# Moving one half of one of eight states between engines in a recurrent-scan and mixture-of-experts kernel

## The reference

```python
def step(state, inp):
    x_t, dt_t, B_t, C_t = inp
    dA = jnp.exp(dt_t[:, :, None] * A[None])
    state = state * dA + (dt_t * x_t)[:, :, None] * B_t[:, None, :]
    y_t = jnp.einsum('bds,bs->bd', state, C_t)
    return (state, y_t)
```

## Time and profile before

| what | us |
|---|---|
| median of 3 runs | 1773.71 |
| lowest, highest | 1764.98, 1775.46 |
| the profiled execution, its time | 1772.78 |
| the profiled execution, its span | 1771.0 |
| DVE busy | 1616.0 (91%) |
| PE busy | 1560.3 (88%) |
| POOL busy | 1440.2 (81%) |
| ACT busy | 1405.2 (79%) |

### The profile page before, as it was taken

One profiled execution on the slowest core, in us unless ns is written; L12 is line 12 of the kernel. 1 busy time (PEld: TensorE's weight loads), 2 busy tenths in 40 slices (PEclk: granted clock), 3 DMA queues, 4 the chain that ended last, 5 costly groups with the idle time before them and its releaser, 6 DMA issues. The chain is left out here.

```text
span 1771.0 us, 43319 instructions
## 1 busy us (share of the span) xinstructions
PE 1560.3 (88%) x13334; PEld 806.2 (46%) x13334; DVE 1616.0 (91%) x1808; ACT 1405.2 (79%) x2640; POOL 1440.2 (81%) x716
## 2 busy tenths in 40 slices
PE   5775589999999999999999999989998989999888
PEld 5422344444444444444544444444444444444444
DVE  5787689999999999999999999999998999999987
ACT  4797587887887788887888788788888788888882
POOL 1365578898988888988898888888998899989976
PEclk9898699999999999999999999999999999999999
DMA  8667656575666775576566566565466454764633
GB/s 240 208 225 220 167 121 139 137 168 167 139 138 139 183 154 134 136 181 158 138 141 162 172 142 135 139 146 145 91 135 157 131 127 97 154 141 107 141 80 79
DMA packets 209432, 261.82 MB, mean 148 GB/s; under 512 B 26826, under 2 KB 105428, under 8 KB 209172
## 3 DMA queue, kind: packets, MB, share of 16 engines
q1 hardware_dynamic: 205236, 252.04, 58.9%
q0 software_dynamic: 4096, 8.40, 1.6%
HBM read 216.32 MB, written 43.79 MB: 147 GB/s over the span
## 5 line engine op out<-in xcount | busy, mean ns | idle before, releaser
L702 POOL TENSOR_TENSOR arena<-arena 128x1024 f32<-128x1024 f32 x512 | 1201.5, 2360 | 201.7 <-DVE arena L1210 160.0
L1210 DVE TENSOR_TENSOR_SCAN arena<-arena,ps 128x512 f32<-128x512 f32 x944 | 1085.7, 1203 | 56.4 <-POOL arena L702 27.2
L961 ACT ACTIVATE arena<-arena,neg_A 128x512 f32<-128x512 f32 (+1 forms) x944 | 630.5, 713 | 88.6 <-DVE arena L1210 84.9
L1418 PE MATMUL ps<-arena 128*64 128x128 f32 x6912 | 471.7, 281 | 118.3 <-DVE arena L1210 92.8
L1432 PE MATMUL ps<-arena,ident 64*64 64x512 f32 x4096 | 559.4, 618 | 1.7 <-POOL arena L702 1.6
L1418 PEld LDWEIGHTS ps<-arena 128*64 128x64 f32 x6912 | 376.1, 138 | 351.8 <-DVE arena L1210 177.6
L1192 DVE TENSOR_TENSOR ps<-arena,ps 128x512 f32<-128x512 f32 x512 | 325.2, 681 | 12.1 <-PE ps L1404 12.0
L967 ACT ACTIVATE arena<-ident,b_turned 128x128 f32<-128x128 f32 x864 | 273.1, 387 | 0.0
L1432 PEld LDWEIGHTS ps<-arena,ident 64*64 64x64 f32 x4096 | 108.0, 132 | 181.9 <-issue 175.1
L902 ACT ACTIVATE arena<-ps,arena 128x256 f32<-128x256 f32 x160 | 67.2, 471 | 112.3 <-PE ps L1502 112.2
L674 POOL DMA_INDIRECT x_rms_by_expert<-arena,slots x64 | 69.4, 1085 | 89.0 <-DMA x_rms_by_expert<-arena,slots 50.0
(11 more groups left out here) (168 smaller groups left out, 1018.6 us busy)
## 6 DMA issues: line engine op xcount, KB each, us to landing
arena<-c_scratch SPq DMA_DIRECT2D x128, 1024.0 KB, 8.6
arena<-w_routed_scaled SPq DMA_DIRECT2D x40, 256.0 KB, 2.8
arena<-in_L_ffn_W_r_dram SPq DMA_DIRECT2D x40, 256.0 KB, 8.9
arena<-c_scratch SPq DMA_DIRECT2D x40, 256.0 KB, 3.5
arena<-w_shared_tiles SPq DMA_DIRECT2D x128, 64.0 KB, 7.8
x_rms_by_expert<-arena SPq DMA_DIRECT2D x1, 5120.0 KB, 27.8
arena<-x_rms_by_expert SPq DMA_DIRECT2D x40, 128.0 KB, 2.6
routed_by_expert<-arena SPq DMA_DIRECT2D x40, 128.0 KB, 8.5
```

The lines of the kernel that those rows point to most:

```text
L702: nc.gpsimd.tensor_tensor(products[:, i % RING, :, :], states[:, i % 2, :, :], c_rows[:, i // CG, i % CG, :].unsqueeze(1).broadcast_to((P, ...
L961: nc.scalar.activation(decay[:, 2 * i + h, :], dflat[:, ds(slot + h * L, L)], ACT.Exp, scale=aflat[:, ds(col, 1)]).then_inc(s["decay_ready ...
L1210: vector.tensor_tensor_scan(states[:, i % 2, h, :], decay[:, m, :], ps[bank][:], 0.0, ALU.mult, ALU.add).then_inc(s["scanned"], 1)
L1418: ins = mm(bank[HP * r:HP * r + HP, c * P:(c + 1) * P], u_turned[:, odd, c, h * P + HP * r:h * P + HP * r + HP], diag[:, c, :], start=True ...
```

## The change

State 5 of a group with blocks gets a new kind Q. Its first half stays as in D: TensorE broadcasts B, VectorE multiplies by u, in place. For its second half GpSimd makes u*B in SBUF (`u_q`, 128x512) after product 3, from a second row of `b_row`, and ScalarE writes the decay to PSUM (`q_decay_to_psum`) after scan (4,0). VectorE thus makes seven products a group with blocks instead of eight. The B rows are laid out by state instead of by group, `c_scratch` gets eight more rows, and a group with a block loads two rows into `b_row` in two DMAs of 256 KB. The load waits for the second product too. `evict_block` moves from step 4 to step 5 of ScalarE's loop. `b_rest` in the first stage moves to other memory, its first write waits for `c_copied` instead of `b_first_made`, and the store of C is two DMAs. The plan of banks for groups with blocks changes by itself: before it was (0,2,1) (1,0,2) (1,2,0) (1,0,2) (2,1,0) (2,0,1) (1,2,0) (0,1,2) and it becomes (2,0,1) (1,2,0) (1,0,2) (1,2,0) (0,1,2) (2,0,1) (1,2,0) (0,1,2).

```diff
-    KIND = ("DEDDEDEE", "DEDDEDEP")
+    KIND = ("DEDDEDEE", "DEDDEQEP")
...
-    DECAYS = (SCANS, SCANS - NH)
+    DECAYS = (SCANS, SCANS - NH - 1)
...
-        b_row = take(L)
+        b_row = take(2 * L, "p (n t) -> p n t", n=2)
+        u_q = take(L)
...
             def store_c(b):
                 sp.wait_ge(s["c_copied"], b + 1)
-                sp.dma_start(c_d[:, b * L:(b + 1) * L], c_new[0:C_B_ROWS, :]).then_inc(s["c_stored"], 16)
+                sp.dma_start(c_d[0:C_B_ROWS, b * L:(b + 1) * L], c_new[0:C_B_ROWS, :]).then_inc(s["c_stored"], 16)
+                sp.dma_start(c_d[C_B_ROWS:, b * L:(b + 1) * L], c_new[Q_ROW:Q_ROW + E, :]).then_inc(s["c_stored"], 16)
...
             def load_b_row(u, g, tb):
                 if not isinstance(u, int) or u:
                     sp.wait_ge(s["u_b_pooled"], u)
-                sp.dma_start(b_row, c_d[S:C_B_ROWS][ds(g, 1), ds(tb, L)].broadcast_to((P, L))).then_inc(s["b_row_loaded"], 16)
+                    sp.wait_ge(s["u_q_pooled"], u)
+                for n in range(2):
+                    sp.dma_start(b_row[:, n, :], c_d[S + n * E:S + (n + 1) * E][ds(g, 1), ds(tb, L)].broadcast_to((P, L))
+                                 ).then_inc(s["b_row_loaded"], 16)
...
-                        pool.wait_ge(s["b_row_loaded"], (b * E + g) * 16 + 16)
+                        pool.wait_ge(s["b_row_loaded"], (b * E + g) * 32 + 32)
...
+                    if blocks and i == Q_AT - 2:
+
+                        nc.gpsimd.tensor_tensor(u_q, u_in.rearrange("p n h t -> p (n h t)")[:, ds(slot_q, L)], b_row[:, 1, :],
+                                                ALU.mult).then_inc(s["u_q_pooled"], 1)
...
-                nc.scalar.copy(c_new, ps[6][0:B_ROW, :]).then_inc(s["c_copied"], 1)
+                nc.scalar.copy(c_new, ps[6][:]).then_inc(s["c_copied"], 1)
...
+            def q_decay_to_psum(u, g, slot):
+
+                act.sem_inc(s["q_bank_claimed"], 1)
+                col = snap(g * SG + (S + Q_AT))
+                nc.scalar.activation(ps[BANKS[True][Q_AT][1]][:], dflat[:, ds(slot + L, L)], ACT.Exp,
+                                     scale=aflat[:, ds(col, 1)]).then_inc(s["q_decay_ready"], 1)
...
-                    if i == 4 and block_before:
+                    if i == Q_AT and block_before:
                         evict_block(u - 1)
...
-                        if KIND[block][i] == "P":
+                        if block_before and (i, h) == (Q_AT - 1, 0):
+                            q_decay_to_psum(*before)
+                        if KIND[block][i] == "P" or (KIND[block][i] == "Q" and h):
                             continue
...
             def first_rest(b):
-                dve.wait_ge(s["b_first_made"], b + 1)
+                dve.wait_ge(s["c_copied"], b + 1)
...
-                        for bank in (held, new):
+                        for bank in (held, new) if KIND[block][i] == "D" else (new,):
                             h = 0 if bank == first else 1
                             vector.tensor_tensor(ps[bank][:], uflat[:, ds(slot + h * L, L)], ps[new][:],
                                                  ALU.mult).then_inc(s["u_b_multiplied"], 1)
...
+                        if KIND[block][i] == "Q" and h:
+                            dve.wait_ge(s["u_q_pooled"], u + 1)
+                            dve.wait_ge(s["q_decay_ready"], u + 1)
+                            vector.tensor_tensor_scan(states[:, i % 2, h, :], ps[bank][:], u_q, 0.0, ALU.mult, ALU.add
+                                                      ).then_inc(s["scanned"], 1)
+                            continue
```

More of the change, by code:

```diff
@@ L58, in mamba_gated_moe @@
     N_SUM = SG
-    KIND = ("DEDDEDEE", "DEDDEDEP")
-    P_AT = SG - 1
-    assert KIND[1].index("P") == P_AT and "P" not in KIND[0]
+    KIND = ("DEDDEDEE", "DEDDEQEP")
+    P_AT, Q_AT = SG - 1, KIND[1].index("Q")
+    assert KIND[1].index("P") == P_AT and not set("PQ") & set(KIND[0])
     D_AT = [[i for i in range(SG) if kind[i] == "D"] for kind in KIND]
@@ L69, in mamba_gated_moe @@
     ND, NE = [len(at) for at in D_AT], [len(at) for at in E_AT]
-    ROW_OF = [i for i in range(SG) if "D" in (KIND[0][i], KIND[1][i])]
+    ROW_OF = [i for i in range(SG) if set("DQ") & {KIND[0][i], KIND[1][i]}]
     COL_OF = E_AT[1] + [i for i in E_AT[0] if i not in E_AT[1]]
@@ L650, in _ @@
             by_g = lambda a: a.rearrange("p h (g i) -> p h g i", g=E)
-            runs = []
             for k, i in enumerate(ROW_OF):
[L653 to L658, removed]
+                nc.gpsimd.tensor_copy(cb_sb[:, :, B_ROW + k * E:B_ROW + (k + 1) * E].unsqueeze(3), by_g(bp_sb[:])[:, :, :, i:i + 1]
                                       ).then_inc(s["bp_parted"], 1)
@@ L664, in _ @@
                                   ).then_inc(s["bp_parted"], 1)
[L665 removed]
+            assert NROW + NE[1] + 1 == N_PARTED
             pool.wait_ge(s["slots_made"], 1)
@@ L693, in gate_attn, with group @@
                 nc.gpsimd.tensor_tensor(s_times_g, gate_silu, attn_in, ALU.mult).then_inc(s["product_s_g_ready"], 1)
-            def group(b, g, blocks, slot=None):
+            def group(b, g, blocks, slot=None, slot_q=None):
                 n = b * S + g * SG
@@ L1184, in group @@
                         dve.wait_ge(s["dt_u_loaded"], b * 32 + 32)
-                    if KIND[block][i] == "D":
-                        k = D_AT[block].index(i)
+                    if KIND[block][i] in "DQ":
+                        k = sum(kind in "DQ" for kind in KIND[block][0:i + 1])
                         new = second if first == held else first
-                        dve.wait_ge(s["b_broadcast"], states_to(u, ND, block, k + 1))
+                        assert KIND[block][i] == "D" or (first, second) == (new, held)
+                        dve.wait_ge(s["b_broadcast"], states_to(u, BROADCASTS, block, k))
                         dve.wait_ge(s["scanned"], m0 + (2 * i + SCANS - 1))
-                        for bank in (held, new):
+                        for bank in (held, new) if KIND[block][i] == "D" else (new,):
                             h = 0 if bank == first else 1
@@ L1202, in group @@
                             continue
[L1203 to L1206, removed]
+                        if KIND[block][i] == "Q" and h:
[4 more added lines that the diff above has]
+                            continue
+                        dve.wait_ge(s["decay_ready"],
+                                    states_to(u, DECAYS, block, m + (0 if block and i > Q_AT else 1)))
+                        if KIND[block][i] in "DQ":
+                            done = PRODUCTS_TO[block][i] - (1 if KIND[block][i] == "D" and bank == held else 0)
+                            dve.wait_ge(s["u_b_multiplied"], states_to(u, PRODUCTS, block, done))
                         else:
@@ L1536, in group @@
                         ahead_g, ahead_t0, ahead_odd = next_g, next_t0, next_odd
-                    if ahead and KIND[ahead[3]][ahead[1]] == "D":
-                        bcast(*ahead, snap(ahead_g * NROW + ROW_OF.index(ahead[1])), ahead_t0)
+                    if ahead and KIND[ahead[3]][ahead[1]] in "DQ":
+                        bcast(*ahead, snap(ahead_g + ROW_OF.index(ahead[1]) * E), ahead_t0)
                     elif ahead and KIND[ahead[3]][ahead[1]] == "E":
```

31 lines of the change are left out of this document (19 added, 12 removed).

## The result

The changed kernel takes 1898.84 us (median of 4, 1890.97 to 1902.44) where the kernel before takes 1774.59 us (4 runs): 1.0708 times as long, 95% interval 1.0676 to 1.0739. The prediction was 1837, with a range of 1812 to 1885. The direction and the place are right, the size is half of what came: 124 us where 63 were summed.

The account below looks back on a forecast made before the run. VectorE is busiest, GpSimd paces half a group, and late half 0 of C closes a loop: 1.7 us in 35 groups (60) plus 3 for four gives 1772.8 + 63 = 1836, median 1837, range 1812 to 1885.

Parts of the forecast that it names:

- what bounds: Groups with blocks: GpSimd sets the pace in the second half; half 0 of C has 3.4 us to spare, loses 4.8.
- VectorE's saved product: VectorE, state 5: saves 0.59 us a group, but by the engines alone only 0.03 is left, 1 us in all.
- hidden: Rival: half 0 of C lands in time for product 0, so no change, 1772 us; chance 12%.
- the loop: GpSimd's product 0 through `u_q`, then the load of C back to product 0: period 25.5 us instead of 23.77.
- The four groups that follow the first group of a sequence: Groups with more slack before product 0: 0.2 us there, no more than 1.7 in any; 3 us taken for the four.
- The new wait for `c_copied`: First stage: met before a wait VectorE already has; with the extra stores nothing to 1 us, taken as 0.
- the landing of half 0 of C: DMA from issue to landing: 8.4 us from one load, plus 0.3 for bytes and burst still in flight.
- the first group: Start of the groups with blocks: no added time in the sum, which counts loads for groups 1 to 39.
- from E to the issue of C: SyncE's queue: E is the end of `u_q`, after product 3; half 0 of C goes out 3.80 us later.
- the burst: Loads undrained ahead of C, with the second row's 256 KB: nothing to 1.5 us, 0.3 taken.
- much slower: Rival: W2 and x also hold up TensorE, or C lands 10.1 us or more after issue: 1913 us; chance 10%.
- The stall by x: ScalarE's `copy_x_block` ahead of the second P decay: late x delays the scan 0.7 us, hidden behind the wait for product 0.

Follow-up runs that it names:

- the row behind C: Changed kernel with the second row of `b_row`, and its wait for `u_q`, loaded behind half 0 of C: 1770.68 us, 1.0007 times the kernel before.
- the wait alone: Kernel before, with the load of `b_row` also waiting for product 3 of the group before, no extra bytes: 1786.1 us, 1.0105 times the kernel before.
- the bytes alone: Kernel before, with a second 256 KB load behind each load of `b_row` and the old wait: 1769.65 us, 1.0003 times the kernel before.
- C ahead of x: Changed kernel, with half 0 of C loaded right behind the `b_row` rows, ahead of x, W1 and its bias: 2127.68 us, 1.2017 times the kernel before.

## Why the prediction was right, and where it was wrong

**Right: what bounds.** That GpSimd sets the pace in half a group, that VectorE's saved product is nearly worthless by itself, and that half 0 of C had less slack than it would lose, all stood. (It had 3.4 us in that group, 3.15 in the median, of which 0.3 pass anyway from landing to product 0; it goes out 5.2 us later, not 4.8.) The version with the row behind C is the rival "hidden" made real: 1771 against its 1772. That they agree so well is luck: 6.6 us gained in the groups pay for some 5 lost in the first, and the rival had neither.

**Right: the loop.** From product 0 to the end of u_q: 12.89 us summed, 12.87 in the group shown. u_q: 1.25 summed, a step of 1.24 (738.75 to 739.99, where product 4 starts). The four groups that follow the first group of a sequence lost 1.8 us together, where 3 was taken from the earlier trace rows. The new wait for `c_copied` and the extra stores cost nothing: the first products of the groups begin at 186.08 us after, 186.20 before.

**What failed** is sizes in the sum, not the mechanism: above all the landing of half 0 of C, put at 8.7 us where it took 9.4, with two smaller terms beside it, and the first group, put at nothing where it cost 6.

**Wrong: from E to the issue of C.** 3.80 summed from the steps in the earlier trace rows, 4.20 measured. Two terms: the step from the bias to C, which the earlier trace rows can't show since C waited there for product 3; I took 0.58 from the step between two other loads, and it is 0.80 (743.42 to 744.22). And E to x, 2.04 summed, is 2.21.

**Wrong, and the largest: the landing.** I took 8.4 and 0.3 for what is still in flight. The median from issue to landing of half 0 is 9.4 us over 39 groups (8.1 to 10.3), where it was 8.7 before (7.2 to 9.6), and 10.0 in the group shown. 8.4 was one load, on the short side. What I gave 0.3 costs 0.7, and the runs say which part of it does: where the same loads go out closer together but without the second row (the wait alone), the landing is 8.8; where the second row goes out behind C and all ahead of C is as before (the row behind C), it is 9.3. So it is the second row's 256 KB, ahead of C or just behind it, and not the tighter burst. x tells the same: 3.8 us after and 2.6 before, in the median, 2.6 with the wait alone and 4.1 with the bytes alone. From landing to product 0 another 0.3 passes, for which I had 0.1.

The sum closes over the 34 groups counted above (means): product 0 to the end of product 3 11.90, u_q 1.24, to the issue of C 4.25, landing 9.38, to product 0 0.32, together 27.09. Summed were 11.64, 1.25, 3.80, 8.7 and 0.1: 25.49. So of 1.6 us that were missing the landing is 0.7, the issue 0.4, the step to product 0 0.2. The last 0.3 is for the most part in five groups, in which GpSimd stands once more between product 0 and product 3, by 1.2 to 1.6 us. In two of them (at 400 and 834 us) VectorE waits for TensorE's fills; TensorE is late there behind x and the fallen clock (below), but no run takes that apart. The bounds were in the prediction (1.5 for the burst, 10.1 for the landing), but each was used alone, as an end of the range with the other at its middle. The time measured, 1899, is nearer to the 1913 of "much slower" than to 1837.

**Wrong: the first group.** I took nothing for it; it costs 6 us (from its first scan to its P scan 46.1 us instead of 40.1). The Q decay of a group is written in ScalarE's loop over the next group, and in the first one that loop starts only after the gelus. VectorE's scan of state 5 waits for it:

```profile
224.29 1.22 DVE L1228 TENSOR_TENSOR_SCAN arena<-ps,arena 128x512 f32<-128x512 f32 x1 [13.38 <-ACT ps L940]
```

Before, that wait was there too, 12.98 us, but at the P scan, with states 5 and 6 already done; now the P scan waits 5.91 us more behind them. The prediction read a steady group and passed over the first, although "one group ahead" is said of ScalarE in the text.

**The stall by x:** summed at 0.7 us and hidden, it is 1.7 in the median (0.8 to 2.3). Hidden it is in the main, since product 0 waits for C behind it; a part of the 0.3 above may be its.

**Two readings of the prediction** are off and change nothing. Between two P scans GpSimd has two gaps of 0.30 to 0.31 us, not three. And a landing of 9.9 gives 2.92 us a group by its own terms, not 2.85, so the upper end would have been 1888.

## What to carry to other kernels

A wait in an in-order load queue belongs to everything behind it: before moving one, list what is queued behind, with its slack, and put the wait behind the last load that has little. Slack makes such costs a threshold: parts that cost nothing and 16 us alone cost 59 together, so a part tested by itself says little of the whole. Take the landing time of a large load from many loads, not from one, and give added bytes beside it a price: 256 KB more cost 1 MB some 0.7 us here. And read the first pass of a software pipeline by itself.

## What the runs showed of the hardware

TensorE's granted clock fell soon after it had stood waiting for x. It was idle for 2.81 us until 745.83; the windows from there show the clock (columns as in the earlier trace rows):

```profile
742.00:746.00 4.00, 1.20 (x11) 0.32 (x10) 3.45 (x3) 0.81 (x2) 3.68 (x3) 1.00 0.69 214
746.00:747.40 1.40, 1.40 (x11) 0.42 (x11) 0.02 (x2) 1.02 (x3) 1.31 (x1) 1.00 0.58 192
747.40:751.00 3.60, 3.60 (x11) 0.66 (x10) 3.57 (x5) 3.58 (x7) 2.32 (x1) 0.53 0.66 122
751.00:755.00 4.00, 4.00 (x48) 2.59 (x44) 3.10 (x4) 1.59 (x4) 0.52 (x2) 1.00 0.87 208
```

For some 3.6 us it is at the lower of the two levels, 1.2 GHz (0.53 on the mean of the window), and two matmuls of 128x512 take 1.91 us there (at 747.44) that took 1.02 before the change (at 733.05). The fills of state 1 come later for it and VectorE waits 0.86 us for them at 754.27. In this group it is hidden, since GpSimd gets C only at 754.51; but the price of a short stall of TensorE need not end with the stall. Over the groups with blocks the clock was 1.00 in the mean before (230 to 1164 us), 0.95 after (235 to 1287), and 0.85 with C ahead of x (235 to 1524), where TensorE stands 9.1 us for x in the median.
